# One fused two-layer sequence kernel: attention makes its scores once

## What is computed

```python
x = _layernorm(x + mamba_both_ways_with_ff(x))   # selective scan, forward and backward, then a feed-forward
x = _layernorm(x + ternary_ffn(x))               # silu(x w1) * (x w2), two gelu layers of 512, down to 128
x = _layernorm(x + attention(x))
x = _layernorm(x + mixture_of_8_experts(x))      # top 2 of 8, each 128 -> 256 -> 128

# attention: 8 heads of 128, 2 groups of keys with 32 latent channels
q = (x @ wq).reshape(Bq, Tq, N_KV, N_REP, HEAD_DIM)
k_lat, v_lat = x @ wk_down, x @ wv_down          # [.., N_KV, 32]
k, v = k_lat @ wk_up, v_lat @ wv_up
scores = jnp.einsum('bqhrd,bkhd->bhrqk', q, k) * scale
scores = jnp.where(causal, scores, jnp.finfo(scores.dtype).min)
y = jnp.einsum('bhrqk,bkhd->bqhrd', jax.nn.softmax(scores, axis=-1), v)
return y.reshape(Bq, Tq, N_HEADS * HEAD_DIM) @ wo
```

## Time and profile before

| | us |
|---|---|
| median of 3 runs | 1955.34 (1953.61 to 1958.84) |
| the profiled execution | 1948.13 |
| its span in the trace | 1946.3 |
| PE / DVE / ACT / POOL busy | 1654.4 / 1541.2 / 1114.8 / 752.7 |
| mean granted PE clock | 0.932 of full |

### The profile page before, as it was taken

One profiled execution on the slowest core, in us unless ns is written; L12 is line 12 of the kernel. 1 busy time (PEld: TensorE's weight loads), 2 busy tenths in 40 slices (PEclk: granted clock), 3 DMA queues, 4 the chain that ended last, 5 costly groups with the idle time before them and its releaser, 6 DMA issues.

```text
span 1946.3 us, 26951 instructions
## 1 busy us (share of the span) xinstructions
PE 1654.4 (85%) x8352; PEld 768.0 (39%) x8352; DVE 1541.2 (79%) x2163; ACT 1114.8 (57%) x1553; POOL 752.7 (39%) x601
## 2 busy tenths in 40 slices
PE   3533588889988999889988999889988999889888
PEld 2200134344444435334444435344444435344545
DVE  3999799779995999779995999779996999631514
ACT  3544486467854885567853885567754884433132
POOL 0455454334632454334632454334533454410102
PEclk7655699999999999999999999999999999989999
DMA  7999998667864896668864796667864896500000
GB/s 187 230 244 248 220 242 203 153 156 199 204 153 121 188 216 163 165 143 196 200 156 118 184 218 163 168 147 198 194 156 112 195 219 165 120 0 0 6 1 6
DMA packets 107915, 309.48 MB, mean 159 GB/s; under 512 B 15970, under 2 KB 32244, under 8 KB 107764
## 3 DMA queue, kind: packets, MB, share of 16 engines
q1 hardware_dynamic: 93556, 279.32, 60.9%
q10 hardware_dynamic: 14208, 28.32, 4.5%
HBM read 287.67 MB, written 19.92 MB: 158 GB/s over the span
## 4 chain that ended last, share of the span: by engine, by line
PE 36%; DVE 28%; issue 13%; ACT 13%; DMA 4%; SPq 2%; ACTq 2%; DVEq 1%; POOL 0%; POOLq 0%
PE ps_pair L716 12%; DVE sb_hst L1295 10%; PE ps_pair L813 7%; DMA sb_ring<-spread_dram 4%; PE ps_pair L872 4%; PE ps_pair L801 4%; DVE ps_in L1287 3%; PE ps_pair L892 3%; ACT sb_mix L1129 3%; DVE sb_nmax L1436 2%; ACT sb_ring L971 2%; ACT L940 2%; DVE sb_u L1339 2%; PE ps_pair L816 1%; DVE sb_eh L1504 1%
## 5 line engine op out<-in xcount | busy, mean ns | idle before, releaser
L1567 POOL TENSOR_TENSOR sb_hc<-sb_hst,sb_crep 128x512 f32<-128x512 f32 x512 | 652.8, 1284 | 916.2 <-DVE sb_hst L1295 642.0
L1295 DVE TENSOR_TENSOR_SCAN sb_hst<-sb_ring,ps_in 128x512 f32<-128x512 f32 x512 | 620.0, 1211 | 5.0 <-ACT sb_ring L971 2.5
L971 ACT ACTIVATE sb_ring<-sb_ring,sb_A 128x512 f32<-128x512 f32 x512 | 344.8, 713 | 207.6 <-DMA sb_ring<-spread_dram 116.9
L1287 DVE TENSOR_TENSOR ps_in<-sb_ring,ps_brow 128x512 f32<-128x512 f32 x512 | 354.4, 692 | 29.5 <-DMA sb_ring<-spread_dram 11.5
L940 ACT ACT_TABLE_LOAD x181 | 232.2, 1283 | 46.4 <-issue 39.4
L872 PE MATMUL ps_pair<-sb_mix,sb_ew 128*128 128x512 f32 x512 | 250.0, 624 | 4.6 <-ACT sb_ea L1163 2.2
L651 PE MATMUL ps_y<-sb_hc,sb_const 128*32 128x512 f32 x1024 | 154.2, 678 | 98.8 <-POOL sb_hc L1567 68.7
L813 PE MATMUL ps_pair<-sb_g,sb_h 128*128 128x512 f32 x320 | 168.6, 652 | 15.8 <-DVE sb_dd L1275 5.1
L801 PE MATMUL ps_pair<-sb_h,sb_g 128*128 128x512 f32 (+3 forms) x512 | 165.0, 452 | 13.1 <-DVE sb_nmax L1436 7.8
L872 PEld LDWEIGHTS ps_pair<-sb_mix,sb_ew 128*128 128x128 f32 x512 | 96.6, 198 | 139.1 <-issue 95.3
L892 PEld LDWEIGHTS ps_pair<-sb_ew,sb_eh 128*128 128x128 f32 x1024 | 121.6, 192 | 26.2 <-issue 17.8
(11 more groups left out here) (219 smaller groups left out, 2065.0 us busy)
## 6 DMA issues: line engine op xcount, KB each, us to landing
sb_ring<-spread_dram SPq DMA_DIRECT2D x512, 512.0 KB, 5.9
spread_dram<-sb_dd ACTq DMA_DIRECT2D x32, 512.0 KB, 3.7
sb_brep<-cut_dram ACTq DMA_DIRECT2D x16, 256.0 KB, 4.1
sb_crep<-cut_dram ACTq DMA_DIRECT2D x16, 256.0 KB, 4.1
sb_xtok<-in_L_attn_x_dram SPq DMA_DIRECT2D x8, 256.0 KB, 6.0
sb_ew<-in_L_ffn_w_dram SPq DMA_DIRECT2D x2, 1024.0 KB, 14.0
out_dram<-sb_yy ACTq DMA_DIRECT2D x8, 256.0 KB, 2.3
sb_h<-in_L_ffn_h_w_dram SPq DMA_DIRECT2D x1, 1024.0 KB, 8.9
```

Of the source, the lines that this page charges most:

```text
L971: act.activation(ring[:, n % RING, 0, :], ring[:, n % RING, 0, :], ACT.Exp, scale=A[d][:, g:g + 1]).then_inc(sem["dA"], 1)
L1287: dve.tensor_tensor(ps_in[n % 2][:], ring[:, n % RING, 1, :], ps_brow[:], ALU.mult).then_inc(sem["dbu"], 1)
L1295: dve.tensor_tensor_scan(hst[:, HST_SLOT[n], :], ring[:, n % RING, 0, :], ps_in[n % 2][:], 0.0, ALU.mult, ALU.add).then_inc(sem["scan"], 1)
L1567: pool.tensor_tensor(hc[:, n % 6, :], hst[:, HST_SLOT[n], :], crep[n // NU][:], ALU.mult).then_inc(sem["hc"], 1)
```

## The change

The 16 score steps and the ten rounds become one list, `ATTENTION`. It takes the pairs of key group and query tile in turn (`GROUPS`: tiles 0 to 3 for the first key group, 3 to 0 for the second). A score step `s` (22 of them, `SCORES`) is one head of tiles 2 and 3, two of tile 1, four of tile 0: PE makes the scores once, with queries in the rows, DVE takes the maxima, ACT takes the exponential of each head with the maximum as its bias and has the row sum written with it (`accum_out`, `zsum`). Eight slots hold exponentials. A step `t` (20) transposes a block of probabilities of four heads by four fp32 transposes of PE (`turn`), ACT copies it (`pT`, three slots), and `values` multiplies it with the latent values one step later. At a step `z` (two) DVE takes the reciprocal of 16 row sums, PE spreads it over rows by 16 small matmuls with the identity, ACT copies it, and at `y` DVE multiplies. The second scores, `pick`, `split`, `mT` and the `ones` matmuls are gone. Banks are no longer taken in pairs: a score or a transposed block takes any free one, and the attention sum holds one.

The strings in `ORDER` and `TURN_ORDER` are written anew for all engines. In the loop body ACT now loads its tables 30 times where it did 25, the first maximum stands behind 49 scan units on DVE where it stood behind 44, and the output's statistics of the previous batch and one gate step stand ahead of attention on DVE where they stood within it.

```diff
+GROUPS = [(k, t) for k in range(KV) for t in (range(TT) if k == 0 else reversed(range(TT)))]
+SCORES = [(k, t, heads) for k, t in GROUPS for heads in {0: [range(REP)], 1: [range(0, 2), range(2, REP)]}.get(t, [[r] for r in range(REP)])]
+TURNS_P = [(k, t, j) for k, t in GROUPS for j in range(t + 1)]
+PSLOT, PTSLOT = 8, 3
...
+    steps = [("s", u) for u in of(SCORES, GROUPS[0])]
+    for n, g in enumerate(GROUPS):
+        ahead = [("s", u) for u in of(SCORES, GROUPS[n + 1])] if n + 1 < len(GROUPS) else []
+        for a, b in itertools.zip_longest(ahead, [("t", x) for x in of(TURNS_P, g)]):
+            steps += [step for step in (a, b) if step]
+        if n + 1 == len(GROUPS) or GROUPS[n + 1][0] != g[0]:
+            steps += [("z", g[0])]
+    for k in range(KV):
+        i = steps.index(("z", k))
+        steps.insert(i + 1, ("y", k))
+    return steps
...
+    for what, i in ATTENTION:
...
+            uses += [[(f"s{i}", "pexp", i + 1)]]
...
+            uses += [[(f"t{i}", "pt", i + 1)]]
...
+            uses += [[(f"zs{i}", "rz", i + 1)]]
...
-        assert name[:3] == "att" or not any(bank in held for bank in mine), name
+        mine = ([bank for bank in lru if bank not in held][0],)
...
 ORDER = dict(
     PE=(
...
-        "xxxxxuxxrxxruxrxhrrxhrurhuxxhrxrrurxhrhrrurxuhhrrurruxxxrxhxhrxhuxrrxhrrrrrrurrrrrrrrrrhrhhuhrurhurxrrhrrrrrru"
...
+        "xxxxxuxxxrxrurhrurhxrurhrhrrurxrrhruruhxrhrruruxrxxrhxxurxruxxxxhxxxhhuxhurrhrhrhrrrrrhrrrrrrrhrrrrrrrrrurrrrr"
...
-                    for k in range(KV):
-                        pe.matmul(ps_pair[i % 2][:, k, 0:(t + 1) * P], qT[:, tl, r, :], kz[:, 2 * k + hf, 0:(t + 1) * P],
-                                  start=True, stop=False)
-                    for k in range(KV):
-                        ins = pe.matmul(ps_pair[i % 2][:, k, t * P:(t + 1) * P], identb[:], maskb[:], start=False, stop=True)
+                    for n, r in enumerate(heads):
+                        pe.matmul(o[:, n * w:(n + 1) * w], qT[:, tl, r, :], kz[:, 2 * k + hf, 0:w], start=True, stop=False)
+                        ins = pe.matmul(o[:, n * w + t * P:(n + 1) * w], identb[:], maskb[:], start=False, stop=True)
                     done(ins)
...
-                def turned_scores(i):
...
-                        pe.matmul(ps_pair[0][:, hf, :], kz[:, 2 * k + hf, j * P:(j + 1) * P],
-                                  qT[:, TILES[hf].index(t), :, :], start=True, stop=False)
...
-                        ins = pe.matmul(ps_pair[0][:, hf, :], pick[:, 2 * k + hf:2 * k + hf + 1].broadcast_to([P, P]), mT[:, TILES[hf].index(t), :, :],
...
+                def turn(x):
+                    k, t, j = TURNS_P[x]
+                    o = claim(f"t{x}")
+                    pe.wait_ge(sem["pexp"], row("pexp", group_scores(k, t)))
+                    for r in range(REP):
+                        slot, at_r = slot_of(k, t, r)
+                        ins = pe.transpose(o[:, r * P:(r + 1) * P], pexp[slot][:, at_r + j * P:at_r + (j + 1) * P], ident)
                     done(ins)
...
+                def values(x):
+                    k, t, j = TURNS_P[x]
+                    if x in FIRST_TURN:
+                        atts[k] = claim(f"att{k}")
                         pe.wait_ge(sem["vlat"], row("vlat", 1))
-                    pe.wait_ge(sem["pexp"], row("pexp", i + 1))
-                    for hf, (t, j) in enumerate(units):
-                        for into, w in ((ps_att, vlat[:, j, k * LAT:(k + 1) * LAT]), (ps_z, ones[:])):
+                    pe.wait_ge(sem["pt"], row("pt", x + 1))
+                    for r in range(REP):
+                        ins = pe.matmul(atts[k][LAT * r:LAT * (r + 1), t * P:(t + 1) * P], vlat[:, j, k * LAT:(k + 1) * LAT],
+                                        pT[:, x % PTSLOT, r * P:(r + 1) * P], start=(j == 0), stop=(j == t))
+                    ins.then_inc(sem["att"], 1)
+
+                for what, i in ATTENTION:
+                    if what == "s":
+                        scores(i)
+                    elif what == "t":
+                        turn(i)
+                        if i >= 1 and i not in FIRST_TURN:
+                            values(i - 1)
+                    elif what == "z":
+                        values(LAST_TURN[i])
+                        o = claim(f"zs{i}")
+                        pe.wait_ge(sem["zr"], row("zr", i + 1))
+                        for t in range(TT):
...
+                                ins = pe.matmul(o[LAT * r:LAT * (r + 1), t * P:(t + 1) * P], zr[:, i, t, r:r + 1].broadcast_to([P, LAT]), ident,
+                                                start=True, stop=True)
+                        done(ins)
...
+                for what, i in ATTENTION:
+                    if what == "s":
+                        k, t, heads = SCORES[i]
+                        w = (t + 1) * P
                         table(EXP_LN)
-                        act.wait_ge(sem["full"], row("full", REST_INDEX[f"e{i}"] + 1))
+                        act.wait_ge(sem["smax"], row("smax", i + 1))
...
-                        act.activation(pexp[i % 3], ps_pair[0][:], ACT.Exp).then_inc(sem["pexp"], 1)
...
-                        act.activation(rz[:], ps_z[:], ACT.Ln).then_inc(sem["lnz"], 1)
-                        act.wait_ge(sem["lnz"], row("lnz", k + 1))
-                        act.activation(rz[:], rz[:], ACT.Exp, scale=-1.0).then_inc(sem["rz"], 1)
+                        if i >= PSLOT:
+                            act.wait_ge(sem["full"], row("full", REST_INDEX[f"t{group_turned(i - PSLOT)}"] + 1))
+                        for n, r in enumerate(heads):
+                            ins = act.activation(pexp[i % PSLOT][:, n * w:(n + 1) * w], bank[tab[f"s{i}"][0][0]][:, n * w:(n + 1) * w], ACT.Exp,
+                                                 bias=nmax[:, k, t, r:r + 1], accum_out=zsum[:, k, t, r:r + 1])
+                        ins.then_inc(sem["pexp"], 1)
...
+                    elif what == "t":
+                        if i >= PTSLOT:
+                            act.wait_ge(sem["att"], row("att", i - PTSLOT + 1))
+                        act.activation(pT[:, i % PTSLOT, :], full(f"t{i}")[:], ACT.Copy).then_inc(sem["pt"], 1)
+                    elif what == "z":
+                        act.wait_ge(sem["yT"], row("yT", i))
...
-                def split(tl):
...
-                    dve.tensor_reduce(nmax[:, tl, r, :, hf], ps_pair[i % 2][:, :, 0:(t + 1) * P], AX.X, ALU.max,
...
+                for what, i in ATTENTION:
+                    if what == "s":
+                        k, t, heads = SCORES[i]
+                        lines = full(f"s{i}")[:, 0:len(heads) * (t + 1) * P].rearrange("p (r n) -> p r n", r=len(heads))
+                        dve.tensor_reduce(nmax[:, k, t, heads[0]:heads[-1] + 1], lines, AX.X, ALU.max, negate=True
+                                          ).then_inc(sem["smax"], 1)
+                    elif what == "z":
+                        dve.wait_ge(sem["pexp"], row("pexp", LAST_SCORE[i] + 1))
+                        dve.reciprocal(zr[:, i].rearrange("p t r -> p (t r)"), zsum[:, i].rearrange("p t r -> p (t r)")
+                                       ).then_inc(sem["zr"], 1)
+                    elif what == "y":
+                        dve.wait_ge(sem["rz"], row("rz", i + 1))
                         dve.wait_ge(sem["stored"], row("stored", 0))
-                        dve.tensor_tensor(yT[k], ps_att, rz[:], ALU.mult).then_inc(sem["yT"], 1)
+                        dve.tensor_tensor(yT[i], use(f"att{i}")[:], rz[:], ALU.mult).then_inc(sem["yT"], 1)
```

184 lines of the change are left out of this document (54 added, 130 removed).

## The result

| | median, us | ratio to the kernel before (95% interval) |
|---|---|---|
| before | 1955.4 (1953.6 to 1958.8) | 1 |
| forecast | 1885 (range 1830 to 1962) | 0.964 |
| after | 1978.0 (1974.7 to 1982.2) | 1.0115 (1.0088 to 1.0141) |

A forecast was written before the change was run, and what follows sets the result against it. First stage bound by DVE and PE about equally, attention by PE's work. Five loop periods -38, period before +13.9 and attention 86.7 to 66, last period -8, flush -17: together -70 from 1948.1, 1878; plus 7.2, 1885 us (1830 to 1962).

The forecast's parts named there:

- the same 6.1 over it: First stage of a loop period: 138.6 us of DVE work plus an unchanged 6.1 left over gives 144.7.
- The products and the tail: DVE idle in attention: 2.0 and 3.0 us before the two products with the reciprocals, 2.6 in the tail.
- item 4: Attention: DVE idle for scores with three free banks, 0.5 to 10.5 us over twelve wide pairs, taken as 6.
- item 5: Attention: the two dt steps wait for ACT behind some three activations of 0.6, 1.9 us of DVE idle.
- PE's work: Per batch on PE: 30.4 us removed, 10.7 added, net 19.7 less, taken as 18.7.
- Costs a little at each switch: PE alternating fp32 scores with bf16 masks per head: the reason for taking 18.7 instead of 19.7 us less.
- the weighed rule: Skill's rule that full clock "doesn't engage" for PE transposes, putting attention often at half clock; prediction held the trace against it.
- the second rival: Second in the prediction's list, B: ACT's queue sets the pace in attention, 1941 us; chance 0.20.
- C: Attention: granted clock falls because PE waits in hand-overs; stage 86 us if 0.6 runs at half clock, time 2041; chance 0.14.
- ACT's work: Per period on ACT: net +13.4 us, row sums taken as 0 extra, plus 6.4 for five more table loads.
- PE's chain alone: Flush attention, without scans: -18.7 of 72.9 us, about +1.5 for the longer hand-over at its end, -17 in all.
- B: Attention: ACT's queue sets the pace, row sums cost extra, exponentials stand behind dt steps; stage 74 us, time 1941; chance 0.20.

The follow-up runs named there:

- run 4: Changed kernel with Identity in place of Silu and Gelu, so ACT loads one table instead of 213: 1956.8 us, ratio 1.0028.
- run 3: Changed kernel with the five ACT activations of the two dt steps in attention cut to 64 of 512 columns: 1976.1 us, ratio 1.0127.
- run 5: Changed kernel with DVE's last read of a dt product taken from SBUF, its bank free at ACT's first activation; measured time not given in the text.
- run 7: Changed kernel with both short dt steps on ACT (64 of 512 columns) and the earlier free bank of dt products: 1943.9 us, ratio 0.9958.
- run 8: Changed kernel whose flush uses the old kernel's order up to the first score, the changed order after it: 1969.1 us, ratio 1.0083.
- run 6: Changed kernel, whole computation, with a dt product's bank not given again within three claims if another is free: 1972.4 and 1976.7 us.

## Why the prediction was wrong, step by step

**DVE's work, right.** 190.5 us a period (138.1 + 52.4) against 189.4; 138.1 of it in the first stage against 138.6, and 1.6 more than forecast in attention.

**The first stage, 144.7 against 147.9.** The work that moved ahead was right; the failed term is "the same 6.1 over it". DVE is idle for 9.2 to 10.4 there. Its waits (633.6 to 781.0):

```profile
DVE ps_brow L1295 <- issue: 3.4, 1, 3.4
DVE sb_dd L1280 <- ACT sb_dd L973: 1.8, 1, 1.8
DVE sb_tick L1284 <- ACT sb_dd L976: 0.7, 1, 0.7
```

Before, the same three were 2.3, 0.4 and 0. These 3.2 us are the miss: 2.1 of them because a dt step now finds ACT late, 1.1 ahead of a copy at the start of the stage, where the profile names no releaser and the cause stays open. With one table (run 4) the last two waits are gone and the first is 3.7, but DVE's own busy time is 139.5, so the stage fell by 1.1 only; why DVE was busy 1.5 us longer in it stays open.

**The products and the tail, right.** 2.2 and 2.1 us before the products (forecast 2.0 and 3.0; the earlier trace rows: 9.64 and 5.96), 2.3 in the tail (2.6).

**The score loop, item 4, wrong: 6 against 13.3** (14.1 and 12.4 in turn). This is 7 of the 8.4 us. I had counted three banks and one score at a time in them, with DVE and ACT at hand. Two things were missing, and the runs size them. First, item 5 booked the dt steps as 1.9 us of DVE waiting for ACT. DVE waited 0.2; the step's real price fell on PE, as 3.8 and 3.0 us for banks and exponentials (runs 3, 5, 7). Second, the sum ran at full clock throughout. The granted clock fell after these waits and, in three periods of five, at the start of the stage: some 3 us (76.2 against 72.5, and 71.1 in run 4, all with the same two waits). With the waits shortened and the clock at 1.00, 66.9 us were left (run 7, period before the loop), 15.6 of them idle time of DVE against the 15.5 that I had summed, though 7.8 of these were for scores and not 6. That is one stage, and its dt steps are cut short on ACT, so it supports the hand-over's size and does not prove it.

**PE's work, 18.7 less forecast.** Busy fell from 201.4 to between 190 and 196 a period, with 189.1 in run 4: some 12 at about the same granted clock as before. "Costs a little at each switch" was a term left at next to nothing. A pair in the changed kernel, at full clock:

```profile
598.53 0.28 PE L838 MATMUL ps_pair<-sb_const,sb_pX 128*128 128x128 f32 x1
598.64 0.49 PE L838 MATMUL ps_pair<-sb_const,sb_mix 128*128 128x128 f32 x3
599.07 0.42 PE L848 MATMUL ps_pair<-sb_pT,sb_vlat 128*32 128x128 f32 x8
599.42 1.12 PE L828 MATMUL ps_pair<-sb_h,sb_g 128*128 128x512 f32 x2
600.38 0.22 PE L829 MATMUL ps_pair<-sb_maskb,sb_identb 128*128 128x128 bf16 x1
600.44 0.28 PE L838 MATMUL ps_pair<-sb_const,sb_pX 128*128 128x128 f32 x1
```

598.53 to 600.44 is 1.91 us; I had 1.7. Four transposes take 0.54 to the values behind them where the earlier trace rows had 0.44 for four in a row, the values 0.35 where I took 0.24. 0.2 a pair is 4 us a batch; the other 2 to 3 of the miss stay open. The transposes themselves did run at full rate: 0.11 from one start to the next (598.53 to 598.64), as in the earlier trace rows. So the weighed rule did not bite here. The prediction says that its time would be that of the second rival; it meant the third, C, the one with the lower clock.

**ACT's work, right in sum.** 162.5 us a period against a forecast of 140.9 + 13.4 + 6.4 = 160.7. The 2.7 us of the row sums, taken as 0, more than cover the difference.

**The flush, -17 against +4.3.** Two steps failed. "PE's chain alone" for attention gave 55.9; it took 65.8. Without scans between, PE waits 6.3 us for exponentials and 4.8 for copies there: the chain is the hand-over, not PE. And I let the stretch ahead of attention stand at 109.6, though the strings were new there as well; it took 121.0. About half of these 11.4 us is the order (run 8), the rest the clock, which was granted at 0.90 here and at 0.95 or 0.96 with the same letters and waits in runs 4 to 7.

**The rivals.** C named the right mechanism, a granted clock that falls because PE is left waiting, but priced it from an assumed share (0.6 of PE's work, stage 86, clock under 0.8). It was 0.87 and 0.92 in the loop. B's stage of 74 came true to half a us, partly by luck. The forecast's own upper end is also given as 74, but items 1 to 5 with the longest wait for banks add up to 70.8. B had half its reasons: exponentials behind dt steps, yes; a full ACT queue, no (49 busy of 74). The likely case would have been B and C small and together, and I gave each its own chance instead. Its effect on the sign was missed too: with the first stage 3 us longer than forecast, a stage of 74 is a loss, since 147.9 + 74.4 is 222.3 against 218.3.
